# Post-norm attention and FFN layer on 8 cores: one PSUM copy split in two, another moved from ScalarE to VectorE

## The reference

```python
qkv = x @ W_qkv.T + b_qkv
q, k, v = jnp.split(qkv, 3, axis=-1)
q = q * scaling
...
attn = jax.nn.softmax(jnp.einsum('bhnld,bhnmd->bhnlm', qb, kb), axis=-1)
out = jnp.einsum('bhnlm,bhnmd->bhnld', attn, vb)
...
x = _layernorm(x + _L0_attn_ref(x, L0_attn_W_qkv, L0_attn_b_qkv, L0_attn_W_out, L0_attn_b_out), axis=-1)
x = _layernorm(x + _L0_ffn_ref(x, L0_ffn_w_gate, L0_ffn_w_up, L0_ffn_w_down), axis=-1)
```

## Time and profile before

| what | us |
|---|---|
| median of 2 runs | 2666.47 (2661.61 to 2671.33) |
| the profiled execution, device time | 2659.09 |
| its span, first to last instruction, slowest core (core 5) | 2657.5 |
| spans of the 8 cores | 2640.4 to 2657.5 |
| mean granted TensorE clock of core 5 | 0.830 |

### The profile page before, as it was taken

One profiled execution on the slowest core, in us unless ns is written; L12 is line 12 of the kernel. 1 busy time (PEld: TensorE's weight loads), 2 busy tenths in 40 slices (PEclk: granted clock), 3 DMA queues, 4 the chain that ended last, 5 costly groups with the idle time before them and its releaser, 6 DMA issues.

```text
span 2657.5 us, 27494 instructions; the slowest of 8 cores (2640.4 to 2657.5 us)
## 1 busy us (share of the span) xinstructions
PE 1998.1 (75%) x10560; PEld 1005.0 (38%) x10560; DVE 757.2 (28%) x1218; ACT 502.0 (19%) x931; POOL 67.1 (3%) x111
## 2 busy tenths in 40 slices
PE   1666219766898678977798678977798678977796
PEld 1443204324443344433443344434443244434342
DVE  2444001043312432143311432133311432133311
ACT  0122101012311222112311122112211222112210
POOL 2100000100000000000000000000000000000000
PEclk9967659977799678978799678987699678988798
DMA  9999995631054002510044102520044102520033
GB/s 183 179 109 121 223 221 169 131 107 32 17 151 133 33 17 88 166 64 32 17 143 127 48 17 88 159 72 32 17 143 127 48 16 75 164 79 17 24 119 111
DMA packets 260175, 253.56 MB, mean 95 GB/s; under 512 B 89952, under 2 KB 223088, under 8 KB 259472
## 3 DMA queue, kind: packets, MB, share of 16 engines
q1 hardware_dynamic: 216576, 121.65, 18.0%
q0 software_dynamic: 19280, 86.11, 14.4%
q10 hardware_dynamic: 24192, 44.05, 5.5%
HBM read 216.13 MB, written 56.62 MB: 103 GB/s over the span
## 4 chain that ended last, share of the span: by engine, by line
PE 62%; DVE 13%; SPq 9%; DMA 6%; another core or an unknown queue 3%; ACT 3%; issue 3%; DVEq 0%; POOL 0%; ACTq 0%; POOLq 0%
PE ps L788 24%; PE ps L843 10%; PE ps L392 8%; SPq L289 8%; PE ps L583 6%; PE ps L426 3%; PE ps L475 3%; PE ps L469 3%; DMA wdb<-wd_nat 2%; DVE attnT L542 2%; SPq L263 1%; DVE x L864 1%; DVE stats L887 1%; DMA wgu<-wuT_s 1%
## 5 line engine op out<-in xcount | busy, mean ns | idle before, releaser
L788 PE MATMUL ps<-x1T,wgu 128*128 128x512 bf16 x3072 | 670.6, 381 | 107.8 <-DMA wgu<-wuT_s 106.3
L788 PEld LDWEIGHTS ps<-x1T,wgu 128*128 128x128 bf16 x3072 | 301.7, 98 | 474.0 <-issue 117.2
L843 PE MATMUL ps<-wdb,hT 128*128 128x512 bf16 x1536 | 339.4, 381 | 27.2 <-DMA wdb<-wd_nat 18.1
L806 DVE TENSOR_TENSOR hT<-silu,ps 128x512 bf16<-128x512 bf16 x192 | 132.1, 688 | 755.9 <-PE ps L788 520.3
L392 PE MATMUL ps<-xT,RWqkv 128*128 128x256 bf16 x2048 | 261.8, 295 | 3.5 <-issue 1.6
L843 PEld LDWEIGHTS ps<-wdb,hT 128*128 128x128 bf16 x1536 | 148.9, 98 | 217.7 <-issue 45.1
L392 PEld LDWEIGHTS ps<-xT,RWqkv 128*128 128x128 bf16 x2048 | 203.4, 105 | 59.2 <-issue 4.7
L800 ACT ACTIVATE silu<-ps 128x512 bf16<-128x512 f32 x192 | 114.8, 598 | 523.8 <-PE ps L788 523.7
L426 PE MATMUL ps<-RWqkv,xT 128*128 128x512 bf16 x512 | 144.3, 433 | 85.5 <-DVE vtok L438 43.3
L583 PE MATMUL ps<-RWout,aoT 128*128 128x512 bf16 x512 | 184.6, 526 | 13.4 <-ACT aoT L570 13.4
L400 ACT ACTIVATE qkT<-ps,bqkvT_s 128x256 bf16<-128x256 f32 x256 | 121.9, 476 | 278.2 <-PE ps L392 277.8
(11 more groups left out here) (71 smaller groups left out, 1098.1 us busy)
## 6 DMA issues: line engine op xcount, KB each, us to landing
wgu<-wgT_s SPq DMA_DIRECT2D x64, 768.0 KB, 5.0
wgu<-wuT_s SPq DMA_DIRECT2D x64, 768.0 KB, 7.0
wdb<-wdT_s ACTq DMA_DIRECT2D x168, 256.0 KB, 2.8
xf<-x POOLq DMA_DIRECT2D x16, 1024.0 KB, 5.3
y<-x POOLq DMA_DIRECT2D x16, 1024.0 KB, 5.6
x<-wqkv POOLq DMA_DIRECT2D x24, 512.0 KB, 8.8
wg_nat<-wg POOLq DMA_DIRECT2D x1, 6144.0 KB, 59.6
wu_nat<-wu POOLq DMA_DIRECT2D x1, 6144.0 KB, 116.5
```

Of the source, the lines that this page charges most:

```text
L788: P.do("tensor", lambda tn, wi=wi, k=k, mi_=mi_, boff=boff, pair=pair: tn.matmul(pair[:, wi * 512:(wi + 1) * 512], wgu[:, boff + wi * (KCH ...
L806: P.do("vector", lambda v, m=m, pair=pair: v.tensor_tensor(hT[:, m * 512:(m + 1) * 512], silu2[:, (m % 2) * 512:(m % 2 + 1) * 512], pair[: ...
L843: P.do("tensor", lambda tn, m=m, l=l, half=half, wslot=wslot, coff=coff: tn.matmul(psl[l][:, half * 512:(half + 1) * 512], hT[:, m * 512 + ...
```

## The change

It does two things in the attention of every tile:

- the copy of 128 x 1024 from PSUM to attnT becomes two VectorE copies of 128 x 512, first half and second half; the first four matmuls of attn_O wait for the first, the last four for the second;
- the copy of 128 x 512 from ps01 to aoT is made by VectorE instead of ScalarE, at the same place of the emission order; those who waited for ScalarE wait for VectorE.

```diff
@@ attn_T @@
-                        P.do("vector", lambda v, pst=pst, eo=eo: v.tensor_copy(
-                            out=attnT[:, eo:eo + 1024], in_=pst[:]),
-                             inc="ve", waits=[("pe", mil["trans", t, st, hh]),
-                                              ("sb11", mil.get("dump_attnT", 0))])
+                        for par2 in range(2):
+                            P.do("vector", lambda v, pst=pst, eo=eo, par2=par2: v.tensor_copy(
+                                out=attnT[:, eo + par2 * 512:eo + (par2 + 1) * 512],
+                                in_=pst[:, par2 * 512:(par2 + 1) * 512]),
+                                inc="ve", waits=([("pe", mil["trans", t, st, hh]),
+                                                  ("sb11", mil.get("dump_attnT", 0))] if par2 == 0 else ()))
+                            mil["attnT_e" if par2 == 0 else "attnT_o", t, st, hh] = P.c["ve"]
@@ attn_O @@
-                                waits=(w + [("ve", mil["attnT", t, st, hh]), ("ve", mil["v_evac", t, st]), ("sc", mil["qk_done", t])]) if i8 == 0 else ())
+                                waits=(w + [("ve", mil["attnT_e", t, st, hh]), ("ve", mil["v_evac", t, st]), ("sc", mil["qk_done", t])]) if i8 == 0
+                                      else ([("ve", mil["attnT_o", t, st, hh])] if i8 == 4 else ()))
...
-                        P.do("scalar", lambda sC, st=st, hh=hh, bank=bank: sC.activation(
+                        P.do("vector", lambda v, st=st, hh=hh, bank=bank: v.tensor_copy(
                             out=aoT[:, hh * 4 * 256:(hh + 1) * 4 * 256].rearrange(
                                 "p (c j) -> p c j", j=256)[:, :, st * 128:st * 128 + 128],
-                            in_=ps01[:, bank * 512:(bank + 1) * 512].rearrange("p (c j) -> p c j", j=128),
-                            func=AF.Copy),
-                            inc="sc", waits=[("pe", mil["out", t, st, hh])])
-                        mil["aoT", t, st, hh] = P.c["sc"]
-                        P.rel("ps01_" + str(bank), "sc")
+                            in_=ps01[:, bank * 512:(bank + 1) * 512].rearrange("p (c j) -> p c j", j=128)),
+                            inc="ve", waits=[("pe", mil["out", t, st, hh])])
+                        mil["aoT", t, st, hh] = P.c["ve"]
+                        P.rel("ps01_" + str(bank), "ve")
@@ wout_st @@
-                    w = P.acq("ps23") + [("sc", mil["aoT", t, st, 1]), ("sc", mil["bcast"]), ("sp3", mil["rwout"])]
+                    w = P.acq("ps23") + [("ve", mil["aoT", t, st, 1]), ("sc", mil["bcast"]), ("sp3", mil["rwout"])]
```

More of the change, by code:

```diff
@@ L637, in tile_front @@
                     P.do("gpsimd", lambda q: q.dma_start(out=dbg_t["d_aoT"], in_=aoT[:]),
-                         inc="sb5", amt=16, waits=[("sc", mil["aoT", DBG_T, 1, 1])])
+                         inc="sb5", amt=16, waits=[("ve", mil["aoT", DBG_T, 1, 1])])
                     mil["dump_aoT"] = 16
@@ L839, in ffn @@
                         w += P.acq("ps01_0") + P.acq("ps01_1") + P.acq("ps23") + P.acq("ps45") + P.acq("ps67")
-                        w += [("sc", mil["aoT", 2 * s + 1, 1, 1]), ("ve", mil["x1t_evac", 2 * s + 1, 1])]
+                        w += [("ve", mil["aoT", 2 * s + 1, 1, 1]), ("ve", mil["x1t_evac", 2 * s + 1, 1])]
                     for l in range(4):
```

## The result

The changed kernel takes 2681.86 us (median of 31 runs) against 2666.67 (30 runs of the kernel before): a ratio of 1.0057, 95% interval 1.0045 to 1.007. That is 15 us more, a clear but small loss, within 2%. The forecast was 2680, from a sum of 15.4 us.

The account below looks back on a forecast made before the run. TensorE was taken to bound the kernel. Per tile 1.01 at W(0) plus 0.09 at W(1) is 1.10, times 14 tiles 15.4 us: 2674.5 on the profiled execution, 2681.9 on the median, forecast 2680, range 2664 to 2701.

Parts of the forecast that it names:

- Which tiles count, what bounds: TensorE carries the chain; tiles 0 and 1 run beside the weight preparation, so 14 of 16 tiles count.
- The 512-column copy, 0.69: A VectorE copy of 512 columns out of PSUM takes 0.69 us, 0.61 from start to start.
- (d): Rival: half copies are cheap (0.61) and the split gains all it can; 8.7 us slower, 2668 to 2675; chance 0.15.
- the low end: Half copies at 0.61 us, 0.57 behind a neighbour; the loss is then 0.62 per tile, or 8.7 us.
- Gain 0.24: Split of attnT, first token half: four matmuls run under the second copy, so A(1,0) starts 0.24 us earlier.
- the place that decides: On VectorE aoT(0,1) stands behind sums and diagonals of A(1,0), so W(0) starts 1.01 us later per tile.
- The tail, 0.09: Second token half: four half copies, then two aoT copies in one queue; W(1) starts 0.09 us later after attnT(1,0).
- The clock, 0: W(0) and W(1) shift nearly equally, one losing what the other gains; effect 0, bounds 16 us either way.
- ScalarE's relief, 0: ScalarE loses 64 aoT copies, 38.0 us, but the chain waited for it only through that copy; worth 0.
- (a): Rival: the stall keeps the clock down through both W steps; over 2% slower, 2723 to 2731; chance 0.05.
- (c): Rival: both W steps long, 31 us slower, 2690 to 2698; chance 0.13 with what lies between it and 2%.
- (b): Rival: no cost, both W steps catch the short form, minus 16 against plus 15.4; 2659 to 2667; chance 0.08.

Follow-up runs that it names:

- e4: Kernel before with attnT copied in two halves, each two even and two odd heads, attn_O ordered in pairs, aoT on ScalarE; ratio 0.9968 to before.
- e2: Kernel before with only the aoT copy moved to VectorE, attnT still one copy; ratio 1.0062 to before.
- e3: Whole change, but VectorE copies aoT(0,1) ahead of the row sums and diagonals of A(1,0); ratio 1.0017 to the kernel before.
- e8: Whole change, plus W starting on aoT of the first head group, waiting for the second ahead of its fifth matmul; ratio 0.9885 to the kernel before.
- e6: Kernel before with one added wait: W(0) waits for the row sums of A(1,1), a stall of 2.68 us per tile; ratio 1.0082 to before.
- e10: Whole change with attnT split by pairs of even and odd heads, and W starting on aoT of the first head group; ratio 0.9883 to before.
- e7: Kernel before with attnT split by pairs of even and odd heads, and W starting on aoT of the first head group; ratio 0.9893 to before.
- e1: Kernel before with only the attnT copy split into first and second half, aoT still on ScalarE; ratio 1.0016 to before.
- e9: Kernel before with only W starting on aoT of the first head group, waiting for the second ahead of its fifth matmul; ratio 0.9878 to before.

## Why the prediction was right

The time came out by the named mechanism. That it came out so close is in part luck: the gain of the split was absent and the clock gave back about as much, and these two errors cancelled.

- **Which tiles count, what bounds.** Right. The 14 tiles behind the preparation carry the loss: rest 2090.2 to 2105.9 is 15.7 us, where 14 x 1.10 = 15.4 was forecast. TensorE's longest wait stayed at 102.3 us.
- **The 512-column copy, 0.69.** Right: 0.681 for attnT, 0.684 for aoT, 2.47 to 2.48 for four in a row (forecast 2.52). Case (d), cheap halves, falls; so does the low end. The estimate of 0.66 from the errata section of the Trainium skill's page "VectorE: DVE Perf Modes" is 3% short.

```profile
L543 DVE CAST attnT<-ps 128x512 bf16<-128x512 f32 x128 | 79.3, 681 | 0.1
...
L574 DVE CAST aoT<-ps 128x512 bf16<-128x512 f32 x64 | 43.7, 684 | 1.0 <-PE ps L565 0.4
```

- **"Gain 0.24: A(1,0) and all behind it start that much earlier."** Wrong. The front went from 19.25 to 19.29. The step took half of 0.65, 0.33, for the four matmuls behind the second copy; they took 0.61. The eight had been two streams side by side, and the split put its wait between them (windows of e4). Even side by side, in e4, four take 0.43, since each matmul lasts some 0.3 from its own start: of the 0.24 at most 0.16 could be had, and e4's front is 19.18.
- **aoT(0,1), "the place that decides".** Right in place and cause (e2 alone has the loss, e3 and e8 remove it). The net was put at 1.01 with the 0.24 already off, a stall of 1.25; it was 1.32 (5.19 less 3.87), and nothing came off.
- **The tail, 0.09.** It was 0.16 (3.95 less 3.79), because the four matmuls behind the last half copy are one stream too: 0.38 from first start to last end in the mean, 0.24 in the sum. e2, with the whole copy, has 0.07.
- **The clock, 0.** W(0) + W(1) went from 13.27 to 13.10, and after W(1) another 0.09 to the end of the x1T copies and 0.34 in each even tile to the next came back, where the time at half clock, from the second residual addition on, fell from 12.3 to 10.2. e6 gives 0.90 back in the W steps. So the term is some -0.4 per tile. "What one W step gains the other lost" holds in both kernels (the two together last 12.7 to 13.5 in each of tiles 2 to 14 on the six cores), but not in e4 and e6 to e10, and it leaves out what the clock does behind W(1). Sum per tile: 0.04 + 1.32 + 0.16 - 0.17 - 0.09 = 1.26, 17.6 us in 14 tiles, less 7 x 0.34, is 15.3.
- **ScalarE's relief, 0.** Right; it lost 36 us of work and the loss is e2's.
- **The rivals.** (a) needed W steps of 16.4; with twice the change's stall e6 had 12.4. (c), both W steps long, occurs in no tile of either kernel. (b), both short, did not come with the change, but e7 to e10 are that state, and worth about what (b) said (13.27 to 12.0, 18 us where it had 16). The advice of the Trainium skill to use both engines for evacuation (page "TensorEngine Tiling (Array Packing)", section on the PSUM bottleneck) is neither borne out nor refuted: e3 has all attnT and aoT copies on VectorE and costs 2.7 us in the rest, while ScalarE goes on emptying other banks.

## What to carry to other kernels

When a copy moves to another engine, ask what stands ahead of it in that engine's list at the moment it is needed; idle shares don't answer that. A wait in the middle of a group of matmuls can break up streams that ran side by side: order the group so that each part holds both (worth 0.18 us per group here). And before making a copy faster, look whether the consumer could start on the part that is ready: three lines did more here (1.2%) than any work on the copies.

## What the runs showed of the hardware that was not expected

- Matmuls that write 64 partitions each, in the two halves of the array's columns, ran side by side although four of one half stood ahead of four of the other in the program: at half clock, starts 0.06 and 0.045 apart by turns in attn_O(0,0) of tile 7, 0.013 and 0.094 in attn_O(0,1), so two streams of 0.107 each. The traces do not say which record is which head, so that the later four overtook the earlier is inferred from the spacing and from e1 and e4.
- A shorter stretch between the two W steps went with a different clock behind it. With 4.91 us from the start of the residual addition to W(1), 5.1 us of W(1) ran at half clock; with 4.07 (e9, where the idle 0.84 just ahead of W(1) is gone) it was 3.0, worth more than the time saved. A longer stall ahead of W(0) (e6) also ended in shorter W steps, with 4.91 in between, so the length of this stretch alone does not settle it; how the clock's rises fall in relation to the two steps was not taken apart further.
